# Last attention of a four-layer block: where the limited bias is added, and when the maximum follows

## The reference

```python
x = x + L3_xattn(layernorm(x), ctx, ctx, mask, attn_bias, ...)

bias   = clip(nan_clamp(attn_bias), -1e4, 1e4)
logits = einsum('bhqd,bhkd->bhqk', q, k) / sqrt(8) + bias
logits = where(mask == 0, -1e4, logits)
probs  = softmax(logits, axis=-1);  probs = where(isnan(probs), 0, probs)
out    = einsum('bhqk,bhkd->bhqd', probs, v) @ W_o.T + b_o
```

## Time and profile before

| | us |
|---|---|
| median of 3 runs | 483.29 (483.26 to 483.6) |
| the profiled execution | 482.26 |
| its span, first to last instruction | 480.4 |
| stage of steps 5 to 7 (397.4 to 414.9), length | 17.50 |
| VectorE, ScalarE, GpSimd busy in that stage | 17.11, 5.61, 4.56 |

### The profile page before, as it was taken

How to read it: one execution, slowest core, us unless ns; L and a number is a source line. 1 busy time by engine, 2 the same in 40 slices (tenths; PEclk the granted TensorE clock), 3 DMA queues, 4 the chain that set the end, 5 groups by cost and what they waited for, 6 DMA issues and landing times.

```text
span 480.4 us, 8622 instructions
## 1 busy us (share of the span) xinstructions
PE 399.9 (83%) x3389; PEld 263.0 (55%) x3389; DVE 366.2 (76%) x811; ACT 247.2 (51%) x424; POOL 108.9 (23%) x95
## 2 busy tenths in 40 slices
PE   4998989999999978884788889899998957878046
PEld 2665556566666657562454446575666723753035
DVE  4799646557454587878779896999898768986985
ACT  3665753333322343561887785855966322534931
POOL 3100000007960010009980444210410133000000
PEclk9999999999999999897999999999999975879759
DMA  7980000000000000071000002000000000000001
GB/s 243 352 278 3 1 1 1 1 0 1 0 1 1 1 2 1 2 299 51 2 1 0 3 1 67 1 1 1 1 1 1 2 0 1 3 0 0 1 0 45
DMA packets 11084, 16.51 MB, mean 34 GB/s; under 512 B 5274, under 2 KB 9764, under 8 KB 10148
## 3 DMA queue, kind: packets, MB, share of 16 engines
q1 hardware_dynamic: 10756, 15.17, 9.0%
q10 hardware_dynamic: 288, 0.79, 0.5%
HBM read 15.43 MB, written 0.52 MB: 33 GB/s over the span
## 4 chain that ended last, share of the span: by engine, by line
PE 50%; DVE 32%; ACT 10%; issue 6%; DMA 1%; POOL 0%; DVEq 0%; ACTq 0%
PE ps L808 7%; PE ps L813 7%; PE ps L847 7%; PE ps L2007 4%; PE ps L241 3%; PE ps L1659 2%; DVE arena L613 2%; PE ps L1997 2%; DVE arena L616 2%; PE ps L2034 2%; PE ps L1645 2%; DVE stats L251 1%; DVE arena L635 1%; DMA ctx_fm<-in_ctx_fm 1%; DVE arena L1800 1%
## 5 line engine op out<-in xcount | busy, mean ns | idle before, releaser
L926 DVE SCALAR_TENSOR_TENSOR arena<-ps,cols,arena 128x512 f32<-128x512 f32 x40 | 29.8, 750 | 42.3 <-PE ps L813 38.0
L822 ACT ACTIVATE arena<-ps,cols 128x512 f32<-128x512 f32 x40 | 27.4, 687 | 63.9 <-PE ps L808 63.9
L241 PE MATMUL ps<-const 128*128 128x256 f32 x158 | 40.6, 407 | 7.4 <-ACT arena L2582 4.4
L1800 DVE TENSOR_SCALAR arena<-ps 128x512 f32<-128x512 f32 x56 | 36.6, 685 | 9.4 <-PE ps L1645 5.4
L847 PEld LDWEIGHTS ps<-weights,arena 128*128 128x128 f32 x320 | 38.6, 192 | 8.1 <-issue 8.0
L241 PEld LDWEIGHTS ps<-const 128*128 128x128 f32 x158 | 30.9, 203 | 15.9 <-ACT arena L2582 4.7
L847 PE MATMUL ps<-weights,arena 128*128 128x128 f32 x320 | 39.2, 276 | 0.2 <-DVE x_tm L915 0.2
L813 PE MATMUL ps<-h_fm,weights 128*128 128x512 f32 x80 | 37.7, 593 | 0.7 <-DVE arena L926 0.7
L808 PE MATMUL ps<-h_fm,weights 128*128 128x512 f32 x80 | 37.7, 594 | 0.6 <-ACT h_fm L382 0.6
L1997 PE MATMUL ps<-h_fm,weights 128*128 128x512 f32 x64 | 30.3, 606 | 2.7 <-ACT arena L2367 1.8
L1645 PE MATMUL ps<-l2buf,picks_b 128*128 128x256 bf16 x160 | 26.7, 286 | 5.1 <-DVE arena L1800 3.7
(11 more groups left out here) (392 smaller groups left out, 884.2 us busy)
## 6 DMA issues: line engine op xcount, KB each, us to landing
weights<-in_moe_w SPq DMA_DIRECT2D x2, 2048.0 KB, 10.0
weights<-in_moe_w SPq DMA_DIRECT2D x3, 1280.0 KB
l2buf<-in_picks SPq DMA_DIRECT2D x1, 1664.0 KB, 8.3
rows<-in_rows SPq DMA_DIRECT2D x1, 1024.0 KB, 13.4
x_tm<-in_x SPq DMA_DIRECT2D x2, 256.0 KB, 5.0
ctx_fm<-in_ctx_fm ACTq DMA_DIRECT2D x1, 512.0 KB, 5.8
ctx_tm<-in_ctx SPq DMA_DIRECT2D x1, 512.0 KB, 14.3
mats<-in_mats SPq DMA_DIRECT2D x1, 512.0 KB, 14.6
```

What stands on the lines that cost most here:

```text
L241: PE.matmul(ps[:, bank, 0:256], ident, const[:, 0:256], start=True, stop=True)
L822: AC.activation(silu[:, k, :], ps[:, k, :], ACT.Silu, bias=bias_col(0, e, k)).then_inc(silu_ok, 1)
L926: V.scalar_tensor_tensor(out=glu[:, u % 2, k, :], in0=ps[:, 2 + k, :], scalar=bias_col(1, e, k), in1=silu[:, k, :], op0=ALU.add, op1=ALU.m ...
L1800: V.tensor_scalar(hat_rows(u, c), ps[:, m % 3, :], 0.0, 1.0, ALU.max, ALU.min).then_inc(near_ok, 1)
```

## The change

For steps 5, 6 and 7 the addition of seen_bias goes from VectorE to GpSimd (a new add_seen_bias), and maximum(t) waits for it. On VectorE weigh_scores(6) now comes ahead of maximum(5); maximum(6) follows divide(3), and maximum(7) and less_last_max follow clear_nan(6) and add(0). On GpSimd the additions for tiles 5 and 6 stand ahead of less_max(5) and less_max(6), and that of tile 7 behind them. TensorE, ScalarE and the DMA queues are as before.

```diff
 # GpSimd
+                def add_seen_bias(t):
+                    pr3 = prob[t % 3].rearrange("p (h k) -> p h k", h=H)
+                    pool.wait_ge(sc_read, 2 * t + 2)
+                    pool_link(G.tensor_tensor(pr3, pr3, seen_bias[t], ALU.add))
+                    bias_added[t] = chained["pool"]
...
-                for t in range(3, NT - 1):
-                    less_max(t)
+                less_max(3)
+                less_max(4)
+                add_seen_bias(5)
+                add_seen_bias(6)
+                less_max(5)
+                less_max(6)
+                add_seen_bias(7)
 # VectorE
-                    dve.wait_ge(sc_read, 2 * t + 2)
-                    dve_link(V.tensor_tensor(pr3, pr3, seen_bias[t], ALU.add))
+                    if t < 5:
+                        dve.wait_ge(sc_read, 2 * t + 2)
+                        dve_link(V.tensor_tensor(pr3, pr3, seen_bias[t], ALU.add))
 
                 def maximum(t):
                     pr3 = prob[t % 3].rearrange("p (h k) -> p h k", h=H)
+                    if t >= 5:
+                        dve.wait_ge(pool_chain, bias_added[t])
...
                 logits(4)
                 clear_nan(3)
-                logits(5)
+                weigh_scores(5)
                 clear_nan(4)
-                logits(6)
+                weigh_scores(6)
+                maximum(5)
+                divide(3)
+                maximum(6)
                 clear_nan(5)
-                divide(3)
-                logits(7)
-                less_last_max()
+                weigh_scores(7)
                 clear_nan(6)
                 add(0)
+                maximum(7)
+                less_last_max()
                 clear_nan(7)
                 divide(4)
                 add_stats(0)
```

More of the change, by code:

```diff
@@ L2143, in experts_and_last_attention @@
             out_bias = []
+            bias_added = {}
             @block.gpsimd
```

## The result

| | before | changed |
|---|---|---|
| median, us | 483.27 (483.2 to 483.6, 4 runs) | 485.79 (485.47 to 486.39, 4 runs) |
| profiled execution, us | 482.26 | 485.52 |
| its span, us | 480.4 | 483.7 |
| first product of tile 5 to first instruction of divide(4), us | 17.32 | 20.33 |

The changed kernel is 2.5 us slower: ratio 1.0057, 95% interval 1.0044 to 1.007. A second set of runs gave 485.97 against 483.23, 1.0059 (1.0038 to 1.0081). The forecast was 486.1, +2.8.

A forecast was written before the change was run, and what follows sets the result against it. VectorE's order was taken as the bound. Some 4.2 us would leave it, but the new schedule's waits put clear_nan(7)'s end at 417.66 against 414.88, +2.8 us: 483.29 + 2.8 = 486.1 us, range 484.3 to 487.2.

The forecast's parts named there:

- The bound before: Stage from 397 to 415 us: VectorE's order bounds it; three additions of 4.05 us in all leave it.
- The exclusion: VectorE's clear_nan or two-SBUF-input operations and GpSimd's operations run one after the other, whoever began first; additions lengthened some 0.38 us.
- rival 2: GpSimd's addition for tile 5 starts ahead of clear_nan(4), margin 0.16 us, and VectorE is held: +4.3 us; chance 0.08.
- The price of the addition: Each seen_bias addition on GpSimd takes 2.36 us, as rows of two full operands do.
- the lower end, 1.90: Each addition on GpSimd takes 1.90 us, as less_max does; the sum is then +1.9 us.
- The path: New schedule through GpSimd's additions, less_max(5), exp(5), keep_turned(4), values(4), project(0), add(0) and maximum(7) to clear_nan(7): +2.8 us.
- all 4 us are given back: At weigh_scores(7), ending at 409.62 against 409.29, the 4 us taken from VectorE are said to be lost again.
- The one term that was off: From the start of values(4) to the end of project(0) 4.65 us on TensorE, then 0.03 until add(0).
- rival 1: Additions at 1.90 us, or TensorE at 2.4 GHz by 408, or both: +0.6 to +1.9 us; chance 0.24.
- The gap that I had named on the other side: TensorE idle about 3 us behind turn(6); at 1.2 GHz after it, values(6) late by 0.4: up to +3.4 us.
- Rival 3: VectorE really relieved: additions at 1.90, no holding, TensorE at 2.4 GHz; +0.1 us, or faster if the clock lasts; chance 0.10.

The follow-up runs named there:

- e_clear4_late: Changed kernel with clear_nan(4) moved behind weigh_scores(6) on VectorE, so GpSimd's addition for tile 5 begins first; 486.79 us against 483.41, ratio 1.0059.
- a_add0_late: Changed kernel with add(0) moved behind maximum(7) and less_last_max on VectorE; 484.73 us against 483.41, ratio 1.0039.
- b_kept_first: Changed kernel with ScalarE's two keep_turned(4) moved ahead of exponential(5); 485.89 us against 483.41, ratio 1.0054.
- d_half_bias: Changed kernel with GpSimd adding only the bias of heads 0 to 7 for tiles 5, 6 and 7; 484.92 us against 483.51, ratio 1.0034.
- j_add6_only: Kernel before with only tile 6's addition on GpSimd, between less_max(5) and less_max(6); 483.2 us against 483.23, ratio 0.9997.
- g_scores5_after: Changed kernel with TensorE's scores(5) moved ahead of turn(3, 0); 483.67 us against 483.51, ratio 0.9998.
- f_scores5_before: Kernel before with TensorE's scores(5) moved ahead of turn(3, 0); 478.98 us against 483.51, ratio 0.9913.

## Why the prediction was right

**The bound before.** VectorE's order, with three additions in it. Right, and the additions did leave (busy 3.8 us less). The premise that the question is when clear_nan(7) ends held too: 65.6 us follow in both.

**The exclusion.** Right in both directions and in its sizes: clear_nan(4) issued 0.16 us ahead of the addition (399.01, 399.17), first and third addition lengthened to 2.75 and 2.74 (2.7 said), clear_nan(5) to 1.29 (1.3 said). e_clear4_late turned the order round and the lengthening went with it. That settles rival 2's mechanism as well: had GpSimd been first, the addition would have been 2.36 us and clear_nan(4) the longer one. Its price was wrong: +4.3 was said; e_clear4_late has the order and costs 0.35 over the changed kernel. I had let weigh_scores(6) stand behind a held clear_nan(4); in the experiment it stands ahead, so this says that the order alone costs nothing, and the case with a held weigh_scores(6) was not tried.

**The price of the addition.** 2.36 taken, 2.35 and 2.36 measured; the lower end, 1.90, was no case here. The estimate of 2.25 from the Trainium skill, "GPSIMD Engine Reference", section 3.1, was 0.1 short.

**The path.** In the changed kernel maximum(5) waited 1.06 us (1.1 said), the wait ahead of clear_nan(5) was 1.64 (1.6), keep_turned(4) ended at 408.38 (408.07 + 0.32 = 408.39), add(0) waited for project(0), 2.79 us (2.5 said). a_add0_late shows that add(0) came last, and that with the addition for tile 7 as the next bound maximum(7) starts 1.1 us earlier; b_kept_first shows ScalarE's order as a link. One reading in the sum was wrong, without changing it: by weigh_scores(7) "all 4 us are given back". Only two of the three additions stand ahead of that step in the kernel before, 2.83 us; what the sum itself gives back by there is these and 0.33 us more (409.62 against 409.29).

**The one term that was off.** From the start of values(4) to the end of add(0)'s wait I had 4.65 + 0.03 us. It was 4.89 (408.44 to 413.33). Values and turn(5) took 0.07 more up to project(0), which took 1.13 instead of 1.06, since the clock rose a little later in that stretch, and the release took 0.10 instead of 0.03. The stage became 3.01 longer instead of 2.8.

**TensorE's clock, the unknown of rival 1.** It did what that rival needed and then undid it: with turn(4) behind values(3) without a gap TensorE rose to 2.4 GHz at about 402 (windows above), turn(4) took 1.62 us, scores(7) 1.42 instead of 2.36. Then it had nothing to do for 4.61 us until keep_turned(4), and was back at 1.2 GHz when values(4) began. The forecast took the low clock for the right stretch for a poorer reason (the long busy stage at 0.59), and it took over from the kernel before how long after the start of values(4) the clock rises, without saying why that should stay. Both came out right partly by luck: in the changed kernel the rise came 3.8 us after that start (3.5 before), in d_half_bias 5.7, and there project(0) was 0.8 us longer. The gap that I had named on the other side, behind turn(6), was 2.96 us; turn(7) took 1.27 and both values ran at 1.2 GHz but for the last products, and this reached nothing: divide(6) starts 3.34 us later than before (422.07, 418.73), no more than divide(4).

**The rivals on the other side.** Rival 3, faster, found no support: j_add6_only gives one addition the most cover that this order has, and gains nothing; g_scores5_after gives tile 5's addition an idle GpSimd, and in the changed order of steps still loses 3.8 us to its counterpart. Two kernels that would close the matter weren't run: the changed order with all additions left on VectorE, which would part the price of the order from that of the move, and g_scores5_after with maximum(5) ahead of clear_nan(4).

**The time.** The profiled execution became 485.52, 485.1 was said; the median 485.79, 486.1 was said. The median's difference is 2.5 and the profiles' 3.3, of which 0.32 is the start of the stage; within the spread of the runs both fit the stage's 3.0.

## What to carry to other kernels

When work is taken from the busiest engine, follow the result that it produces, not the engine's load: here an addition of 1.22 us on VectorE became one of 2.35 on GpSimd, or 2.75 with a clear_nan beside it, and two of them stood in a queue ahead of an operation (less_max) that other engines were waiting for. Before splitting the work of a full engine, look at what it waits for just ahead of the full stretch: moving one step of TensorE ahead of a step that had to wait gave VectorE its work 5.5 us earlier and made the stage 3.6 us shorter, with the same operations on VectorE. And where an order is changed, ask of each step that now stands ahead of a critical one (add(0), exponential(5)) when its own input comes.

## What the runs showed of the hardware that I had not expected

TensorE's granted clock moved the result by the place of its rise rather than by its mean. The same project(0) took 1.06 us before, 1.13 in the changed kernel, 1.53 in e_clear4_late and 1.91 and 1.92 in b_kept_first and d_half_bias. In the last, 0.8 of 2.0 us gained upstream was lost so. Behind a gap of 4.61 us TensorE ran at 1.2 GHz again, and so it did behind the 2.82 us in b_kept_first: there the values at 405.46 were fast and turn(5) behind the gap slow. The length of the gap doesn't decide it alone. In d_half_bias TensorE stood for 2.89 us ahead of turn(7), and turn(7) went at 2.4 GHz, in 1.09 us; what decides is not shown by these runs.

```profile
419.40 1.09 PE L2049 MATMUL ps<-const,arena 128*128 128x128 f32 x8 [2.89 <-DVE arena L2278]
```

A VectorE operation that is held shows no wait. clear_nan(4) in f_scores5_before has a bracket of 0.55 us for exponential(4) and a duration of 1.98 instead of 0.68; the 1.3 us that it stood for GpSimd are in its duration. Whoever reads the waits alone doesn't find the contention; it is found by comparing the durations of one form.
